# Routing of a mixture of experts: the low one-hots move to GpSimd, one scan serves all experts, both choices' slots are worked out together

## What is computed

```
probs = jax.nn.softmax(x @ gate_w.T, axis=-1)
top2_w, top2_idx = jax.lax.top_k(probs, 2)
a_e = top2_idx.reshape(-1)
counts = jnp.bincount(a_e, length=E)
valid = (counts <= cap)[a_e]
onehot = jax.nn.one_hot(a_e, E, dtype=jnp.int32)
pos = jnp.take_along_axis(jnp.cumsum(onehot, axis=0) - 1, a_e[:, None], axis=1)[:, 0]
```

## Time and profile before

| | us |
|---|---|
| median of 3 runs | 1922.46 (1920.78 to 1922.85) |
| profiled execution, its time | 1918.8 |
| its span, first to last instruction | 1917.0 |
| TensorE busy | 1690.9 (88%) |
| VectorE busy | 1142.3 (60%) |
| ScalarE busy | 893.3 (47%) |
| GpSimd busy | 394.9 (21%) |

### The profile page before, as it was taken

How to read it: one execution, slowest core, us unless ns; L and a number is a source line. 1 busy time by engine, 2 the same in 40 slices (tenths; PEclk the granted TensorE clock), 3 DMA queues, 4 the chain that set the end, 5 groups by cost and what they waited for, 6 DMA issues and landing times. The chain is left out here.

```text
span 1917.0 us, 38671 instructions
## 1 busy us (share of the span) xinstructions
PE 1690.9 (88%) x11908; PEld 1094.2 (57%) x11909; DVE 1142.3 (60%) x2436; ACT 893.3 (47%) x1523; POOL 394.9 (21%) x559
## 2 busy tenths in 40 slices
PE   8999999999999999998489999999999399934771
PEld 4523434344434444436379999999999357923551
DVE  5688898989898999858821111111111487887224
ACT  4437777677677776771023333333333252230233
POOL 2310000000010000040023333333333100001782
PEclk9979999999999999999789999999999699977896
DMA  6501222212222221426735666665666200034545
GB/s 212 183 24 49 57 57 58 56 56 56 59 57 59 55 59 56 129 55 185 258 113 168 186 169 187 171 184 169 186 168 186 94 1 1 1 131 136 71 53 176
DMA packets 118378, 207.52 MB, mean 108 GB/s; under 512 B 22064, under 2 KB 88176, under 8 KB 108848
## 3 DMA queue, kind: packets, MB, share of 16 engines
q1 hardware_dynamic: 89280, 171.29, 28.1%
q0 software_dynamic: 20352, 22.92, 7.4%
q10 hardware_dynamic: 8688, 12.58, 1.9%
HBM read 163.65 MB, written 56.10 MB: 115 GB/s over the span
## 5 line engine op out<-in xcount | busy, mean ns | idle before, releaser
L607 DVE TENSOR_REDUCE unit_max<-ps_ring 128x1 f32<-128x512 f32 x1024 | 640.3, 684 | 76.8 <-PE ps_ring L500 70.5
L593 ACT ACTIVATE w<-ps_scores 128x1024 f32<-128x1024 f32 x512 | 498.1, 1022 | 237.5 <-PE ps_scores L562 237.4
L500 PE MATMUL ps_ring<-k_stack,q_stack 96*128 96x512 bf16 x1024 | 359.2, 392 | 10.6 <-POOL v_padded L458 7.9
L562 PE MATMUL ps_scores<-q_stack,k_stack 98*128 98x512 bf16 x1024 | 306.4, 381 | 2.6 <-ACT w L593 2.5
L1475 PEld LDWEIGHTS m_ps_h<-m_xt,w1s 128*128 128x128 f32 x2272 | 267.2, 193 | 4.6 <-issue 0.9
L1475 PE MATMUL m_ps_h<-m_xt,w1s 128*128 128x128 f32 x2272 | 267.6, 276 | 0.6 <-issue 0.6
L1485 PE MATMUL m_ps_y<-w,m_ht 128*128 x1136 | 260.8, 383 | 0.0
L522 PE MATMUL ps_o<-w,v_padded 128*32 128x256 f32 x4096 | 260.6, 383 | 0.0
L500 PEld LDWEIGHTS ps_ring<-k_stack,q_stack 96*128 96x128 bf16 x1024 | 98.6, 96 | 253.7 <-DVE unit_max L607 181.4
L1485 PEld LDWEIGHTS m_ps_y<-w,m_ht 128*128 128x128 f32 x1136 | 210.1, 190 | 29.5 <-issue 0.2
L1507 ACT ACTIVATE m_ht<-m_ps_h,w1s 128x128 f32<-128x128 f32 x568 | 162.4, 368 | 97.0 <-PE m_ps_h L1475 97.0
(11 more groups left out here) (258 smaller groups left out, 1540.9 us busy)
## 6 DMA issues: line engine op xcount, KB each, us to landing
w1s<-in_w SPq DMA_DIRECT2D x71, 1028.0 KB, 4.9
o_raw<-o_transposed SPq DMA_DIRECT2D x64, 128.0 KB
rows<-g_rows SPq DMA_DIRECT2D x16, 512.0 KB, 4.6
y<-sums SPq DMA_DIRECT2D x16, 512.0 KB, 6.5
q_parts<-qk_part SPq DMA_DIRECT2D x16, 384.0 KB, 2.8
k_parts<-qk_part SPq DMA_DIRECT2D x16, 384.0 KB, 2.8
q_stack<-q_parts SPq DMA_DIRECT2D x64, 96.0 KB
k_stack<-k_parts SPq DMA_DIRECT2D x64, 96.0 KB
```

Source lines behind the costliest of these rows:

```text
L500: nc.tensor.matmul(out[:, :], qs[0:STACK, u, qt * P:(qt + 1) * P], ks[0:STACK, u, half * HALF:(half + 1) * HALF], start=True, stop=True).t ...
L562: mm = nc.tensor.matmul(p_s[kt % 2][:, half * HALF:(half + 1) * HALF], ks[:, u, kt * P:(kt + 1) * P], qs[:, u, half * HALF:(half + 1) * HALF],
L593: nc.scalar.activation(pt[:, kt, :], p_s[kt % 2][:, :], ACT.Exp, scale=SCALE)\
L607: nc.vector.tensor_reduce(unit_max[:, u % 2, half, qt:qt + 1], src[:, :], axis=AX.X, op=ALU.max).then_inc(ring_used, count)
```

## The change

GpSimd now makes the low one-hots: 64 comparisons of 128 x 128 (`low_onehots`), each with a pointer scalar, into four buffers of eight instead of two. In the first routing stage it makes all eight groups, in the second seven (`on_pool`), and VectorE makes the last as before. The eight scans become one over 256 elements, with the totals laid out expert by expert and a factor of 0 at each expert's first column to start anew. The slots of both choices are worked out in one row of instructions. The mask is written as bf16 by the addition itself. Tokens and gains are written where they are needed, without copies. The map loop is written out in full.

```diff
-        names = ("ex", "pr", "pr2", "eq", "cand", "oh1", "oh2", "mask", "incl", "pos", "prod")
+        names = ("ex", "pr", "pr2", "eq", "cand", "pos")
-        oh_lo = [mem.sb(f"e_oh_lo{h}", [P, 2, DEEP // 2, P]) for h in range(2)]
+        LOS, LO_BUFS = 2 * NT // DEEP, 4
+        oh_lo = [mem.sb(f"e_oh_lo{h}", [P, 2, DEEP // 2, P]) for h in range(LO_BUFS)]
+        on_pool = LOS if tiles > P // 2 else LOS - 1
+        def low_onehots(m):
+            for k in range(2):
+                for j in range(DEEP // 2):
+                    i = m * (DEEP // 2) + j
+                    last = nc.gpsimd.tensor_scalar(oh_lo[m % LO_BUFS][:, k, j, :], iota_p[:, :], lo[:, k, i:i + 1], None,
+                                             ALU.is_equal)
+            return last
...
-                nc.gpsimd.iota(token[:, :], pattern=[[P, NT]], base=-N, channel_multiplier=1, **imprecise)\
-                    .then_inc(made, 1)
+                for k in range(2):
+                    nc.gpsimd.iota(value[:, k, :, 0], pattern=[[P, NT]], base=-N, channel_multiplier=1, **imprecise)\
+                        .then_inc(made, 1)
+                nc.gpsimd.memset(resets[:, :, :], 1.0).then_inc(made, 1)
...
+                nc.gpsimd.memset(resets[:, :, 0:1], 0.0).then_inc(made, 1)
...
+                pool.wait_ge(lo_ready, 1)
+                for m in range(on_pool):
+                    if m >= LO_BUFS:
+                        pool.wait_ge(mapped, (m - LO_BUFS + 1) * DEEP)
+                    low_onehots(m).then_inc(lo_made, 1)
...
-                link(v.memset(unit[:, :], 1.0))
...
-                link(v.tensor_tensor(t["mask"][:, :, :], t["oh1"][:, :, :], t["oh2"][:, :, :], ALU.add))
-                v.tensor_copy(maskb[:, :], t["mask"][:, :, :].rearrange("p i e -> p (i e)")).then_inc(mask_done, 1)
+                v.tensor_tensor(maskb[:, :].rearrange("p (i e) -> p i e", e=E), oh1, oh2, ALU.add).then_inc(mask_done, 1)
...
-                link(v.tensor_copy(totals[:, :, :].rearrange("p i e -> p (i e)"), p_n[:, 0:G]))
-                for e in range(E):
-                    scan = v.tensor_tensor_scan(out=t["incl"][:, :, e], data0=unit[:, :], data1=totals[:, :, e],
-                                                initial=0.0, op0=ALU.mult, op1=ALU.add)
-                    link(scan)
+                link(v.tensor_copy(totals[:, :, :], p_n[:, 0:G].rearrange("p (i e) -> p e i", e=E)))
+                link(v.tensor_tensor_scan(out=incl[:, :, :].rearrange("p e i -> p (e i)"),
+                                          data0=resets[:, :, :].rearrange("p e i -> p (e i)"),
+                                          data1=totals[:, :, :].rearrange("p e i -> p (e i)"),
+                                          initial=0.0, op0=ALU.mult, op1=ALU.add))
+                v.tensor_tensor(totals[:, :, :], incl[:, :, :], totals[:, :, :], ALU.subtract)
...
+                v.scalar_tensor_tensor(out=lo[:, :, :], in0=hi[:, :, :], scalar=-float(P), in1=slot[:, :, :],
+                                       op0=ALU.mult, op1=ALU.add).then_inc(lo_ready, 1)
...
+                for m in range(LOS):
+                    if m >= on_pool:
+                        dve.wait_ge(mapped, (m - LO_BUFS + 1) * DEEP)
+                        shape, i0 = [P, 2, DEEP // 2, P], m * (DEEP // 2)
+                        v.tensor_tensor(oh_lo[m % LO_BUFS][:, :, :, :],
+                                        bcast(iota_p[:, :].unsqueeze(1).unsqueeze(1), shape),
+                                        bcast(lo[:, :, i0:i0 + DEEP // 2].unsqueeze(3), shape),
+                                        ALU.is_equal).then_inc(lo_last, 1)
+                    for at in range(DEEP):
+                        i, k, u = m * (DEEP // 2) + at // 2, at % 2, m % 2 * DEEP + at
+                        wait_from(dve, mapped, m * DEEP + at - 2 * DEEP + 1)
+                        v.scalar_tensor_tensor(
+                            out=oh_hi[u], in0=bcast(iota_t[:, :].unsqueeze(1), [P, 2, tiles]),
+                            scalar=hi[:, k, i:i + 1],
+                            in1=bcast(value[:, k, i, :].unsqueeze(2), [P, 2, tiles]),
+                            op0=ALU.is_equal, op1=ALU.mult).then_inc(hi_done, 1)
...
+                for m in range(LOS):
+                    if m < on_pool:
+                        pe.wait_ge(lo_made, m + 1)
+                    else:
+                        pe.wait_ge(lo_last, m - on_pool + 1)
+                    for at in range(DEEP):
+                        n = m * DEEP + at
+                        pe.wait_ge(hi_done, n + 1)
```

More of the change, by code:

```diff
@@ L971, in stage_route @@
         iota_t = mem.sb("e_iota_t", [P, tiles])
-        token = mem.sb("e_token", [P, NT])
-        small = {n: mem.sb(f"e_{n}", [P, NT]) for n in ("mx", "sm", "rc", "w1", "w2", "cm", "slot")}
-        sloti = mem.sb("e_sloti", [P, NT], I32)
-        hi_i = mem.sb("e_hi_i", [P, NT], I32)
+        small = {n: mem.sb(f"e_{n}", [P, NT]) for n in ("mx", "sm", "rc", "cm")}
+        sloti = mem.sb("e_sloti", [P, 2, NT], I32)
+        hi_i = mem.sb("e_hi_i", [P, 2, NT], I32)
         hi = mem.sb("e_hi", [P, 2, NT])
@@ L1065, in _ @@
                 link(v.tensor_tensor(t["pr"][:, :, :], t["ex"][:, :, :], wide(small["rc"]), ALU.mult))
-                dve.wait_ge(made, 7)
-                link(v.tensor_reduce(small["w1"][:, :], t["pr"][:, :, :], axis=AX.X, op=ALU.max))
-                first_of(t["pr"][:, :, :], small["w1"], t["oh1"])
-                link(v.scalar_tensor_tensor(out=t["pr2"][:, :, :], in0=t["oh1"][:, :, :], scalar=-2.0,
+                gains, oh1, oh2 = [value[:, k, :, 1] for k in range(2)], oh12[:, 0, :, :], oh12[:, 1, :, :]
@@ L1071, in _ @@
+                dve.wait_ge(made, 10)
+                link(v.tensor_reduce(gains[0], t["pr"][:, :, :], axis=AX.X, op=ALU.max))
+                first_of(t["pr"][:, :, :], gains[0], oh1)
+                link(v.scalar_tensor_tensor(out=t["pr2"][:, :, :], in0=oh1, scalar=-2.0,
                                             in1=t["pr"][:, :, :], op0=ALU.mult, op1=ALU.add))
-                link(v.tensor_reduce(small["w2"][:, :], t["pr2"][:, :, :], axis=AX.X, op=ALU.max))
-                first_of(t["pr2"][:, :, :], small["w2"], t["oh2"])
@@ L1087, in _ @@
+                v.tensor_tensor(totals[:, :, :], incl[:, :, :], totals[:, :, :], ALU.subtract)
+                count = incl[:, :, NT - 1]
                 if fixed is None:
@@ L1123, in _ @@
                 v.tensor_copy(c.owner[:, 0:owners], ownf[:, :]).then_inc(owned, 1)
-                for k, gain in enumerate((small["w1"], small["w2"])):
-                    link(v.tensor_copy(value[:, k, :, 0], token[:, :]))
-                    link(v.tensor_copy(value[:, k, :, 1], gain[:, :]))
-                def outer_products(g, first, last):
-                    for u in range(2 * DEEP):
-                        h, at = u // DEEP, u % DEEP
-                        i0 = g * DEEP + h * (DEEP // 2)
-                        i, k = i0 + at // 2, at % 2
-                        if at == 0:
-                            wait_from(dve, mapped, g * (2 * DEEP) + (h - 1) * DEEP)
-                            shape = [P, 2, DEEP // 2, P]
-                            v.tensor_tensor(oh_lo[h][:, :, :, :],
-                                            bcast(iota_p[:, :].unsqueeze(1).unsqueeze(1), shape),
-                                            bcast(lo[:, :, bass.ds(i0, DEEP // 2)].unsqueeze(3), shape), ALU.is_equal)
+                for m in range(LOS):
[9 more added lines that the diff above has]
+                        wait_from(dve, mapped, m * DEEP + at - 2 * DEEP + 1)
@@ L1146, in outer_products @@
                             op0=ALU.is_equal, op1=ALU.mult).then_inc(hi_done, 1)
-                peeled_ends(dve, NT // DEEP, outer_products)
                 dve.wait_ge(mapped, 2 * NT)
@@ L1162, in _ @@
                     pe.wait_ge(padded, len(hi_flat))
-                def outer_products(g, first, last):
-                    for u in range(2 * DEEP):
-                        pe.wait_ge(hi_done, g * (2 * DEEP) + u + 1)
-                        nc.tensor.matmul(p_m[:, 0:COLS], oh_lo[u // DEEP][:, u % 2, u % DEEP // 2, :],
-                                         hi_flat[u][:, :],
-                                         start=(first and u == 0), stop=(last and u == 2 * DEEP - 1)).then_inc(mapped, 1)
-                peeled_ends(pe, NT // DEEP, outer_products)
+                for m in range(LOS):
[6 more added lines that the diff above has]
+                        pe.wait_ge(hi_done, n + 1)
+                        nc.tensor.matmul(p_m[:, 0:COLS], oh_lo[m % LO_BUFS][:, at % 2, at // 2, :],
+                                         hi_flat[m % 2 * DEEP + at][:, :],
+                                         start=(n == 0), stop=(n == 2 * NT - 1)).then_inc(mapped, 1)
         mem.clear()
```

47 lines of the change are left out of this document (24 added, 23 removed).

## The result

The changed kernel takes 1944.05 us (median of 4 runs, 1942.88 to 1946.14) against 1922.39 us in the same session: ratio 1.0125, 95% interval 1.0112 to 1.0139. It is slower by about 22 us; the forecast was 1910.9. The profiled execution took 1944.12 us around a span of 1942.3, and the one before lay 3.6 us under its median, so the two spans differ by 25.3 us and the medians by 21.7.

The account below looks back on a forecast made before the run. VectorE was taken to bound both routing stages. Gains of 6.0 (preparation), 4.4 and 1.5 (maps) less 0.3 make 11.6 us: 1907.2 profiled, 1910.9 as median; the range takes in 1903.8 below and reaches 1922.

Parts of the forecast that it names:

- The bound: Both routing stages: VectorE works without a gap while the rest waits; a stage ending x earlier shortens the kernel by x.
- Before the slots: Preparation on VectorE alone, before slots are known: fewer instructions gain 3.0 us a stage, 6.0 in all, between 5.5 and 6.8.
- I count nothing: Preparation: GpSimd's extra iota and two memsets finish before VectorE needs them; if late, some 0.1 us would be lost.
- The price of a comparison: Map loop on GpSimd: one 128x128 comparison takes 333 to 489 ns, lower taken; step 0.283 us with 0.06 overlap.
- the upper end: GpSimd comparison priced like a two-input addition, 2.13 ns an element: 489 ns, a step of 0.44 us.
- The cycle: Map loop: GpSimd and VectorE streams alternate, 0.345 us per comparison in the first stage, 0.31 in the second.
- the prediction's own sum: Both stages' maps, c being the cycle: 9.0 + 120c = 54.4 + 5.7 at break-even, a cycle of 0.43 us.
- Behind the last comparison: End of each map, last comparison to table copy: 2.7 us in the first stage, 4.35 in the second.
- The clears: Stage end: GpSimd clears 15 semaphores instead of 12 before its first gather, 0.05 us each, 0.15 a stage lost.
- The third: Rival, map loop: the comparison is dear, 2.13 ns an element, stages 34.3 and 30.2 us, 1926.9 us; chance 0.08.
- The first: Rival, map loop: no contention between GpSimd and VectorE, step 0.283 us, 18.7 us gained, 1903.8 us; chance 0.18.
- the second: Rival, map loop: whole instructions of both engines alternate, 0.56 and 0.493 us a pair, +10.7, 1933.2 us; chance 0.07.

## Why the prediction was wrong

**The bound.** Right. VectorE's row of instructions set the end of the map before, and what a stage lost came out at the end: 12.4 + 15.5 - 5.8 and two later gathers (below) make 22.6 us against 21.7 between the medians. The list of waits didn't say all that was read from it: of TensorE's 17.7 us the 12.7 of the longest lie ahead of the first one-hot. The loads that ended by 950 us before end later now, with a DMA share of 0.75 from 950 to 955 us in the windows below, but still long before the map.

**Before the slots.** Right: 3.0 us a stage were forecast, 2.7 and 3.2 came. The scan of 256 took 0.69 us (0.70 forecast), product and reduction 0.69 each, the small ones 0.20. Two small things were missed. In the first stage VectorE waited 0.25 us for the triangle, since GpSimd's constants are more now ("I count nothing", with the 0.1 us for the case named there); and the addition that reads the ranks from PSUM takes 0.58, not 0.43. The one that read them before took 0.42 as well; the new one reads the totals expert by expert, out of their order, and whether that is the cause was not tested. The run with all one-hots on VectorE agrees with the part: 0.9957, 8.3 us (5.4 to 11.3), where 6.0 for the preparation and 1.7 for the copies were in the working.

**The price of a comparison: the step that failed.** The prediction had both ends from rows, 333 and 489 ns, and wrote: "I take the lower one, because a comparison with a scalar reads one tensor as the cast does." It measured 583 ns from one start to the next with VectorE idle, 596 in duration, where the forecast had steps of 283 and 440 (0.06 us of overlap make 273 and 429 of its own figures; the slip of 0.01 us changes nothing). Not only the choice was wrong: the upper end was too low as well. The number of tensors read isn't what sets the price; a product of two tensors is cheaper (0.41) than a comparison of one with a scalar (0.58), and a copy (0.24) is in a class of its own. The Trainium skill ("GPSIMD Engine Reference", Engine selection) gives one-input operations as roughly line-rate and two-input ones as about twice slower than on VectorE; for this shape the one-input comparison is the dearer of the two on GpSimd (0.58 against 0.41), far from line-rate with 4.66 us a group against 1.14 on VectorE, and the measurement decides. The row for 8 elements was a good base: 233 + 120 x 2.5 = 533 ns, and with a constant as scalar a comparison's mean was 527. What was low in the upper end was the slope, 2.13 where it is 2.5 ns an element (44 ns too little), the pointer scalar, taken as 0.03 us, which costs 0.09 in the step, and the overlap, taken as 0.06 us from memsets, which is 0.013 here.

**The cycle.** The working of the streams that alternate gave 0.345 and 0.31 us. Measured are 0.622 and 0.608 over the stage. 0.583 of that is GpSimd alone and 0.03 to 0.04 contention, on average; but GpSimd was disturbed only part of the time, because VectorE stood waiting for it. Where neither waits, the step is 0.67 to 0.96 us. Put into the prediction's own sum, 120 x 0.615 + 9.0 - 54.4 - 5.7 = +22.7 us gives 1945.2, and 1944.05 was measured. The frame held; one term was mis-sized, by 0.28 us in the first stage and 0.30 in the second, 120 times in all. That the sum meets the median within 1.2 us is partly luck: the 9.0 holds 1.6 us for waits at VectorE's wide comparisons that the measured steps already contain, and what the ends of the stages took beyond the forecast, 1.0 us behind the last comparison and 0.2 for the clears (next two points), is missing from it.

**Behind the last comparison.** First stage 2.3 us from there to the table copy (2.7 forecast), second 5.8 (4.35 forecast). For parts of the map TensorE ran at a lower granted clock than the 1.00 of before at 950 to 955 (2.4 GHz; 0.50 is the lower level, 1.2 GHz), though in those same 5 us it had 1.00 now as well. Ahead of the stretch at 0.50 it had waited up to 2.8 us between groups for the comparisons; that these waits lowered the clock is not shown. The windows of after, with the clock in the third column from the right:

```profile
core 0: us, PE busy (x) PEld busy (x) DVE busy (x) ACT busy (x) POOL busy (x), PEclk, DMA share, GB/s
950.00:955.00 5.00, 2.33 (x17) 1.99 (x16) 3.52 (x10) 0.00 (x0) 5.00 (x9) 1.00 0.75 240
961.00:970.00 9.00, 8.15 (x32) 7.47 (x32) 6.08 (x16) 0.00 (x0) 9.00 (x16) 0.50 0.01 2
...
1780.00:1788.00 8.00, 7.08 (x39) 6.59 (x38) 1.38 (x6) 0.00 (x0) 2.22 (x4) 0.61 0.00 0
```

In the window from 961 it doesn't matter, as the products still end before the next group of one-hots. In the last, 16 products are left when GpSimd is done, TensorE is busy 7.08 of 8 us at 0.61, and it sets the end: they take 5.68 us, and at the 2.05 for eight of the row at 1762.62 they would take 4.1. That is the likely place of the 1.4 us; it was not tested by itself.

**The clears.** 0.15 us a stage were forecast for three more; from table copy to first gather it is 3.44 us now and 3.16 before, 0.28; in the second stage 3.10 and 2.89, 0.21. In the first stage 12 clears started between 965.3 and 966.0 us before and 15 between 978.8 and 979.8 now, about 0.07 us each, where the forecast had 0.05.

**The rivals.** The third was right in kind ("the comparison is dear") and had 0.08; its number, 1926.9, was too low because it used the upper end above. The first and the second are out: an undisturbed comparison was never 0.28 us, and with VectorE idle, or with its iotas in PSUM, it is as long as in the changed kernel, so taking turns can't be what makes it long. The sign that the text named for rival 3, long comparisons "even where VectorE stands still", is what the trace shows, with 0.58 us in place of 0.45.

## What to carry to other kernels

Before work moves to an engine, measure there the very instruction, in its form, with its kind of scalar and its size; a neighbour in the trace with the same number of inputs was off by a factor of two. If none can be measured, don't pick the end of the range that makes the change pay, and ask first how many times longer the work is on the new engine: here 4.66 against 1.14 us a group, which pays for three of eight groups, once the two engines don't disturb each other, and not for all. A helper engine should get the share that it ends before it is waited for, and the main engine's operands should be where the two don't meet.

## What was not expected of the hardware

- On GpSimd a tensor with a scalar costs 2.5 ns an element in f32 and 0.583 us at 128 x 128; two tensors 0.41; a copy 0.24; a pointer scalar 0.09 more than a constant.
- With one of VectorE's two operands in PSUM, GpSimd runs undisturbed (9.30 us for 16, as alone) and VectorE's step is no longer (0.273 against 0.277 us).
- Two unbroken streams with SBUF operands slow each other: GpSimd by 15 to 23% beside high one-hots of 142 columns (10.65 to 11.45 us against 9.30) and VectorE by 13 to 16% (12.58 to 12.91 against 11.1), in the kernel by up to 65% for GpSimd (7.70 against 4.66 us a group); and in one way of starting them, in five of five phases, GpSimd's instruction waits some 13 us for the end of VectorE's run.
